# Two transformer blocks with cross attention on one core: GpSimd puts a group's rows of maxima ahead of its other work of the same beat

## The reference, cut to what matters

```
h1 = _ln(x, n1_g, n1_b)
x = _attn(h1, h1, q1, k1, v1, o1_w, o1_b, heads) + x
h2 = _ln(x, n2_g, n2_b)
x = _attn(h2, context, q2, k2, v2, o2_w, o2_b, heads) + x
h3 = _ln(x, n3_g, n3_b)
a, g = jnp.split(h3 @ ff_w1 + ff_b1, 2, axis=-1)
return a * jax.nn.gelu(g, approximate=False) @ ff_w2 + ff_b2 + x
```

## Time and profile before

| | |
|---|---|
| time, median of 3 runs | 3364.1 us (3362.29 to 3372.93) |
| the profiled execution's own time | 3361.17 us |
| its span, first to last instruction | 3359.3 us |
| PE busy (matmuls) | 3061.1 us, 91% of the span |
| DVE busy | 2045.8 us, 61% |
| ACT busy | 1897.1 us, 56% |
| POOL busy | 729.0 us, 22% |
| granted TensorE clock, mean | 0.961 of full speed |

### The profile page before, as it was taken

One profiled execution on the slowest core, in us unless ns is written; L12 is line 12 of the kernel. 1 busy time (PEld: TensorE's weight loads), 2 busy tenths in 40 slices (PEclk: granted clock), 3 DMA queues, 4 the chain that ended last, 5 costly groups with the idle time before them and its releaser, 6 DMA issues.

```text
span 3359.3 us, 43794 instructions
## 1 busy us (share of the span) xinstructions
PE 3061.1 (91%) x16000; PEld 1418.0 (42%) x16000; DVE 2045.8 (61%) x2732; ACT 1897.1 (56%) x3646; POOL 729.0 (22%) x972
## 2 busy tenths in 40 slices
PE   4887888989899999999999999999999999998998
PEld 1342333334345443544345343454434543443445
DVE  5555556667656676657666676566666665566621
ACT  1543546656574566646674565745666466646641
POOL 2332222312312233022320323121230013002010
PEclk8997989999999999999999999999999999999999
DMA  6443434534433435424343434333343214322212
GB/s 160 130 111 86 120 87 122 154 90 108 120 104 97 128 80 153 112 86 125 96 128 82 129 102 125 105 91 106 77 134 101 73 41 138 91 47 50 74 38 79
DMA packets 208597, 342.27 MB, mean 102 GB/s; under 512 B 25464, under 2 KB 107776, under 8 KB 207104
## 3 DMA queue, kind: packets, MB, share of 16 engines
q1 hardware_dynamic: 203264, 338.09, 36.3%
q0 software_dynamic: 5120, 1.39, 0.3%
HBM read 202.29 MB, written 114.75 MB: 94 GB/s over the span
## 4 chain that ended last, share of the span: by engine, by line
PE 67%; DVE 12%; DMA 6%; ACT 6%; POOL 4%; issue 3%; SPq 2%; DVEq 0%; ACTq 0%; POOLq 0%
PE pr L1303 15%; PE po L1320 14%; DVE mx L1111 8%; PE pd L1287 7%; PE pf L1170 5%; PE pf L1223 5%; PE pf L1236 4%; PE pf L1193 4%; PE pf L1211 3%; ACT ET L1020 3%; PE pf L1202 3%; DVE DEN L1119 3%; DMA QS<-MT 2%; PE pf L1228 2%; DMA WS<-parts 1%
## 5 line engine op out<-in xcount | busy, mean ns | idle before, releaser
L1020 ACT ACTIVATE ET<-pr 128x512 f32<-128x512 f32 (+1 forms) x2720 | 1478.4, 597 | 1268.4 <-PE pr L1303 1256.4
L1111 DVE TENSOR_REDUCE mx<-pd 128x2 f32<-128x800 f32 (+2 forms) x1600 | 1592.6, 1030 | 914.3 <-PE pd L1287 911.8
L1303 PE MATMUL pr<-QS,KS 64*128 64x512 f32 (+1 forms) x2720 | 857.2, 502 | 100.8 <-DMA QS<-MT 55.5
L1320 PE MATMUL po<-ET,V 128*32 128x512 f32 (+2 forms) x5440 | 748.8, 624 | 0.7 <-ACT OU L1026 0.7
L1303 PEld LDWEIGHTS pr<-QS,KS 64*128 64x128 f32 (+1 forms) x2720 | 342.5, 184 | 939.5 <-ACT ET L1020 654.0
L1287 PE MATMUL pd<-KS,QS 64*128 64x400 f32 (+2 forms) x3200 | 612.4, 372 | 107.1 <-DVE mx L1111 88.8
L1287 PEld LDWEIGHTS pd<-KS,QS 64*128 64x128 f32 x3200 | 370.9, 191 | 188.9 <-DVE mx L1111 141.0
L896 POOL TENSOR_TENSOR HS<-uT,HS 128x512 fp32r<-128x512 f32 (+4 forms) x168 | 190.0, 1131 | 607.6 <-ACT uT L984 607.6
L913 POOL DMA_DIRECT2D QS<-MT x160 | 93.8, 588 | 953.6 <-DVE MT L1135 950.7
L1223 PE MATMUL pf<-HS,WS 128*128 128x512 f32 x665 | 191.2, 417 | 11.5 <-issue 8.9
L1320 PEld LDWEIGHTS po<-ET,V 128*32 128x32 f32 (+2 forms) x5440 | 106.9, 108 | 203.5 <-issue 197.6
(11 more groups left out here) (81 smaller groups left out, 2060.0 us busy)
## 6 DMA issues: line engine op xcount, KB each, us to landing
WS<-parts SPq DMA_DIRECT2D x160, 320.0 KB, 3.0
QS<-scr_q SPq DMA_DIRECT2D x80, 512.0 KB, 5.6
scr_k<-HS SPq DMA_DIRECT2D x144, 200.0 KB
scr_q<-HS SPq DMA_DIRECT2D x96, 256.0 KB
KS<-scr_k SPq DMA_DIRECT2D x80, 300.8 KB, 5.2
KS<-scr_k SPq DMA_DIRECT2D x80, 300.0 KB, 6.1
KS<-scr_k SPq DMA_DIRECT2D x80, 192.0 KB, 4.8
scr_k<-HS SPq DMA_DIRECT2D x48, 256.0 KB
```

What stands on the lines that cost most here:

```text
L1020: activation(ET[0:q.rows[k], s % 2, 2 * pair + e, :], pr[e][0:q.rows[k], :], ACT.Exp).then_inc(score_free, 1)
L1111: v.reduce_max(mx[q.kind][:, t, 2 * p:2 * p + 2, c], pd[no % 2][:, :, 0:cols], AX_X).then_inc(unit_free, 1)
L1303: mm(pr[e][0:m, :], keys, queries, start=True, stop=True).then_inc(score_ready, 1)
L1320: ins = mm(po[32 * h:32 * h + own.shape[1], :], own, ET[0:m, s % 2, h, :], start=k == 0, stop=k == q.kt - 1)
```

## The change

In POOL's loop over the beats the loop over `PUT_AT` stands ahead of the loop over `PLACES` instead of behind it. Nothing else is changed: the beats, the transfers, the semaphores and the other four streams (PE, DVE, ACT, SP) are the same instruction for instruction.

```
             for beat in range(FIRST_BEAT, BEATS + BEATS_BEHIND + 1):
+                for q in PUT_AT.get(beat, []):
+                    put_maxima(q)
                 for p in PLACES.get(beat, []):
                     beside(*p)
                 if beat == FIRST_BEAT:
                     put_maxima(GROUPS[0])
-                for q in PUT_AT.get(beat, []):
-                    put_maxima(q)
                 if ended_slot(beat, DIVIDE, DIVIDE_ALONE):
                     divide(ended_slot(beat, DIVIDE, DIVIDE_ALONE))
```

## The result

| | before | after |
|---|---|---|
| median of 14 runs each | 3372.4 us (3354.2 to 3386.1) | 3356.1 us (3337.7 to 3363.9) |
| ratio to before | | 0.9952, 95% interval 0.9932 to 0.9971 |
| the profiled execution's own time | 3361.2 us | 3362.8 us |
| granted clock, mean | 0.961 | 0.960 |

The change makes the kernel 16 us faster (10 to 23), not 53. The spread of single executions is as large as that: the profiled one of before is one of the fastest of its 14, that of after one of the slowest, so the two traces have the same length. They are read here for where time goes, and the medians for how much.

What follows compares the result with a forecast made beforehand. PE was taken as the bound, busy 3061.1 of 3359.3 us. Savings of 35 (waits) + 18 (clock) = 53 us off 3361.2 gave 3308, plus 2 for the median: 3310 us, range 3294 to 3334.

Steps and rivals of the forecast that it cites:

- How much earlier the puts go, and what is left of the waits: At groups' first scores, earlier puts on POOL shrink PE's eleven waits of 39.7 us, saving 35 (25.0 to 39.7).
- What a wait costs in clock: PE runs at low clock in or behind the ten larger waits; shortening them saves 18 us more (10 to 28).
- What is held up: POOL's split work behind the moved puts is delayed about 8 us; cost put at nothing, at most 8 us.
- the rival in which the gain is given back: PE runs into waits for DVE or ACT, or SP's stores set the landing; 3355 to 3370 us, chance 0.07.
- The slower rival: POOL stands at L913 for late maxima while a split waits; 3384 us with holds of 4 us, chance 0.05.
- The first rival: PE's waits for the maxima go but the clock doesn't come back; 3328 us, chance 0.08.

Runs made afterwards that it cites:

- the first experiments: The first four experiments, run in one series in which the kernel before had a median of 3367.8 us.
- all wide stores: Key and query stores each as one run of equal pitch, with query loads changed: 3309.8 us on the kernel before, 3281.9 us on the changed kernel.
- a fourth one: Each split's high part stored once more to a tensor nobody reads: 3481.4 us on the kernel before, 3468.6 us on the changed kernel.
- keys wide: Key stores alone as one run of rows of equal pitch: 3349.2 us on the kernel before, 3319.3 us on the changed kernel.

## Why the prediction was wrong

The direction held, and 3310 us with a range from 3294 to 3334 did not: 3356. Point by point:

**How much earlier the puts go, and what is left of the waits: right.** 35 us were forecast. The eleven waits shrank from 39.7 to 3.0 us. The sum over all groups fell by 33.3, because group 50, whose put didn't move, now waits 3.4 us: its pair landed after 9.9 us instead of 6.0. The lead over before falls there from 15.1 to 8.4 us in the two traces.

**What a wait costs in clock: the right price, but not kept.** Groups 20 and 24 gained 2.0 and 2.9 us beside their waits. Over the whole trace the 18 us of this term are not there: (1 - 0.960) x 2 x 3361.0 = 269 us at the lower level (0.50), against 262. New waits behind the old ones brought new low stretches, as from 876 to 886 us behind group 24. The trace of before is one of its better executions, though: over fourteen executions of each, those of before taken from the series of the first experiments, the mean clock is 0.957 and 0.960, some 20 us less at the lower level, where the term wanted 66 (75 x 35/39.7). So part of it came, less than a third. Where nothing is given back the price holds: on all wide stores the mean clock rose from 0.965 to 0.972, and 17.0 us less of waiting made the profiled execution 30.6 us shorter, 1.8 us for each (1.3 to 1.6 by the ratios and the medians). The prediction's 53 for 35 is 1.5.

**What is held up, put "at nothing", and the rival in which the gain is given back, 0.07: this is the step that failed.** The sum takes nothing off for waits that stand behind the stalls. In the traces PE's new waits are 10.4 us for its bank, 7.5 for DVE, 4.1 for `ET` and 3.1 for a load of queries, 25 us in all, and its idle time fell by 4.0 us instead of 35. I looked for the cover in what POOL delays and for the loss in DVE (61%) and ACT (56%), whose shares leave room. PE does wait for these two, as the rival said, and the time is in the rival's range; but what holds them is not their own work, it is a transfer: the stores of splits before ACT, the outputs before DVE. In this form the stores ran at a DMA share near 0.52. From 906 to 910 us of before that moved 172 GB/s, by which the three stores of a key split of 200 KB each take 3.6 us (an estimate), and the key projections follow each other at some 4 us. By the runs, the stall at the first scores had in part been time in which they drained. The rival had the stores in it, but only as what sets the put's landing. Three rows could have told: ACT's 4.4 us of waits for `scr_k<-HS` in before, small but already above zero, DVE's 34.6 us for `OA<-OU`, and SP's queue right behind group 24, where fifteen stores of keys follow each other from 894.37 us on.

The four pairs of kernels say it in one table. The yield is the time won by the change, by the medians, over what PE's wait for the maxima lost in the two traces:

| stores of splits | wait for maxima, us | ACT's wait for stores, us | PE's wait for its bank (L1193), us | DVE's wait for `OA<-OU`, us | change worth, us | yield |
|---|---|---|---|---|---|---|
| a fourth one | 55.5 to 18.3 | 56.0 to 74.3 | 13.3 to 39.0 | 96.0 to 89.6 | 12.8 | 0.34 |
| as they are | 55.5 to 22.2 | 4.6 to 28.6 | 3.4 to 13.8 | 34.6 to 47.3 | 16.3 | 0.49 |
| keys wide | 44.9 to 21.7 | 0.7 to 20.4 | 3.2 to 19.7 | 27.3 to 28.5 | 29.8 | 1.28 |
| all wide | 30.6 to 13.6 | 0 to 0.6 | 3.0 to 3.0 | 26.4 to 26.9 | 27.9 | 1.64 |

The first two rows differ by less than the spread of the executions, and by the ratios the last is 22.6 us and 1.33. What stands clear is the step from the second row to the third: the same change is worth more where the key stores are faster (337 GB/s from 882.5 to 884 us of the kernel before with wide keys, against 172 above), with less waiting to win. With all stores fast it is worth at least as much as on the old layout for half the waiting. The third row doesn't follow from the ring alone, for its waits of ACT and of PE for the bank grow nearly as on the old layout or more.

**Other points.** The slower rival, POOL standing at the put while a split waits, did not come: POOL stands 79 us longer at L913 than before, and ACT's new waits for its ring are all for stores. The first rival, low clock with no wait in front, has no run of its own; the low stretch behind group 24 has a wait of 2.41 us in front. What stays open is how the loss divides between the ring and the outputs: no run made the ring deeper or gave `OA<-OU` a way past the stores, and that these transfers land late because of the key stores rests on their wait growing by 12.7 us on the old layout and by 1.2 with wide keys. Open, too, is why group 50's pair landed so late in that one execution.

## What to carry to other kernels

Before a stall is priced, look at what drains during it: a ring of buffers, a queue of stores. If a wait on such a resource is already above zero near the stall, the stall may partly be the same time under another name, and the gain is then what that resource has to spare, not the length of the stall. Here the engines' shares did not show this. The waits of the engines that stand at the resource gave a hint (4.4 and 34.6 us), and making it slower and faster and watching what the same change is worth gave the answer.

## What was not expected of the hardware

In these traces the form of the far side of a store set its speed. Stores of 128 rows to 8 heads x 16 rows hold the DMA share near 0.52 (from 906 to 910 us of before), those of 64 rows to 4 heads near 0.26 (from 885.5 to 887 us; 0.25 from 927 to 931); with one pitch over all 128 rows the stores of queries reach 0.91 (from 837.1 to 839.4 us with all stores wide). One stretch with query stores in the kernel before:

```profile
872.50:878.40 5.90, 2.14 (x12) 0.34 (x10) 1.35 (x2) 2.04 (x4) 1.63 (x2) 0.94 0.56 194
```

and one in the kernel before with all stores wide:

```profile
837.10:839.40 2.30, 2.30 (x16) 0.81 (x17) 1.51 (x4) 1.43 (x3) 0.00 (x0) 1.00 0.91 341
```

194 and 341 GB/s. Times 16 engines the shares 0.52, 0.26 and 0.91 make some 8, 4 and 15 of them (estimates); how many engines carried a store no run shows. Together with the new loads of queries the new form was worth 62 us without the change, and with it about 74 (the 90 less the 16.3 of the change alone), more than anything the order of POOL's work could give.
